# Turning the three-part maximum with a transposing DMA instead of TensorE transposes and a ScalarE copy

## The reference

```
x = x + 0.5 * ffn(layernorm(x))        # 8 routed experts, top 2, plus one shared expert
x = x + attention(layernorm(x))        # causal, linear position bias, softmax
x = x + 0.5 * ffn(layernorm(x))
```

## Time and profile before

| What | Value |
|---|---|
| Runs | 319.05 us median, 316.27 to 319.38 |
| The profiled execution's own time | 317.94 us |
| Its span, first to last instruction | 316.2 us |
| Granted TensorE clock, mean | 0.968 |
| PE busy | 286.5 us, 91% |
| DVE busy | 251.3 us, 79% |
| ACT busy | 175.6 us, 56% |
| POOL busy | 127.7 us, 40% |
| Data moved by DMA | 17.73 MB |

### The profile page before, as it was taken

The page is one execution under the profiler, slowest core; times in us unless marked ns, Lnnn a source line. Parts: engine busy times, 40 slices in busy tenths (PEclk is TensorE's granted clock), DMA queues, the critical chain, the costliest instruction groups (busy, mean ns, idle before and its releaser), DMA issues.

```text
span 316.2 us, 7140 instructions
## 1 busy us (share of the span) xinstructions
PE 286.5 (91%) x2328; PEld 185.6 (59%) x2328; DVE 251.3 (79%) x1039; ACT 175.6 (56%) x342; POOL 127.7 (40%) x251
## 2 busy tenths in 40 slices
PE   0889998999998898999799999999999999999994
PEld 0688886977664343334433344333443799989994
DVE  3799898889787787998778989998621698988875
ACT  2423433433555777878578888886888333334330
POOL 1355256306128623575324534666533352420200
PEclk9999999999997599999889999997999999999999
DMA  6910000660022113411113411110000001000011
GB/s 169 244 24 2 0 0 4 224 167 11 3 101 100 42 51 116 151 54 53 51 40 127 140 54 52 54 55 1 4 2 2 0 3 33 2 18 20 1 32 35
DMA packets 20668, 17.73 MB, mean 56 GB/s; under 512 B 2460, under 2 KB 19420, under 8 KB 20572
## 3 DMA queue, kind: packets, MB, share of 16 engines
q1 hardware_dynamic: 19912, 17.05, 18.0%
q10 hardware_dynamic: 720, 0.23, 0.4%
HBM read 9.74 MB, written 7.34 MB: 54 GB/s over the span
## 4 chain that ended last, share of the span: by engine, by line
PE 61%; DVE 14%; POOL 9%; issue 8%; ACT 4%; DMA 2%; SPq 1%; DVEq 0%; POOLq 0%
PE bank L904 16%; PE bank L1033 10%; PE bank L1001 8%; PE bank L839 6%; PE bank L841 5%; PE bank L840 5%; DVE X L699 4%; POOL probs L402 3%; DVE masked_s L767 2%; PE bank L974 2%; DMA X<-in_x 2%; DVE stats L622 2%; PE bank L1043 2%; ACT probs L528 2%; PE bank L1056 2%
## 5 line engine op out<-in xcount | busy, mean ns | idle before, releaser
L767 DVE CUSTOM_DVE_ANT_0 masked_s<-bank,causal_sb 128x512 f32<-128x512 f32 (+3 forms) x256 | 110.0, 486 | 16.0 <-PE bank L974 15.8
L528 ACT ACTIVATE probs<-bank 128x512 f32<-128x512 f32 x160 | 89.7, 602 | 26.0 <-PE bank L1001 25.1
L699 DVE SCALAR_TENSOR_TENSOR X<-bank,coef,X 128x128 f32<-128x128 f32 x272 | 76.2, 342 | 16.2 <-PE bank L904 13.2
L904 PEld LDWEIGHTS bank<-w_sb,act 128*128 128x128 f32 x512 | 67.3, 192 | 6.6 <-ACT act L451 1.1
L904 PE MATMUL bank<-w_sb,act 128*128 128x128 f32 x512 | 67.7, 275 | 0.6 <-ACT act L451 0.6
L402 POOL TENSOR_SCALAR_AFFINE_SELECT probs<-probs 128x512 f32<-128x512 f32 x64 | 39.8, 635 | 65.5 <-ACT probs L528 65.5
L974 PE MATMUL bank<-KA,QA 54*128 54x512 bf16 (+3 forms) x256 | 59.0, 318 | 4.8 <-DVE smax L767 4.1
L451 ACT ACTIVATE act<-bank 128x512 f32<-128x512 f32 x72 | 41.7, 594 | 37.3 <-PE bank L841 36.7
L1001 PE MATMUL bank<-QA,KA 57*128 57x128 bf16 (+3 forms) x256 | 59.3, 317 | 0.9 <-issue 0.7
L1033 PE MATMUL bank<-probs,VA 128*32 128x256 f32 (+2 forms) x640 | 53.6, 403 | 1.4 <-issue 0.9
L839 PE MATMUL bank<-XH,w_hi 128*128 128x512 f32 x88 | 42.3, 481 | 3.0 <-DVE gated L684 1.8
(11 more groups left out here) (87 smaller groups left out, 334.4 us busy)
## 6 DMA issues: line engine op xcount, KB each, us to landing
qk_scratch<-qk_parts SPq DMA_DIRECT2D x8, 384.0 KB, 2.6
QA<-qk_scratch SPq DMA_DIRECT2D x32, 96.0 KB, 2.2
KA<-qk_scratch SPq DMA_DIRECT2D x32, 96.0 KB, 2.3
qk_scratch<-qk_parts SPq DMA_DIRECT2D x8, 256.0 KB, 2.9
qk_scratch<-qk_parts SPq DMA_DIRECT2D x8, 128.0 KB, 2.8
QA<-smaxT SPq DMA_DIRECT2D x64, 3.0 KB
out_x<-X SPq DMA_DIRECT2D x4, 256.0 KB, 2.3
X<-in_x SPq DMA_DIRECT2D x3, 256.0 KB, 6.1
```

The costliest lines, as they stand in the source:

```text
L528: nc.scalar.activation(dst, src, ACT.Exp).then_inc(exp_done, 1)
L699: m = nc.vector.scalar_tensor_tensor(X[:, b * NT + t, :], Y_BANK[i % 3][:, t * P:(t + 1) * P], coef[:, j % 2, t, n:n + 1], X[:, b * NT + t ...
L767: r = nc.vector.tensor_tensor_reduce(masked_s[:, u % 4, off:off + n], bank[:, off:off + n], causal_sb[:, S - n:S], 1.0, -3e38, ALU.add, AL ...
L904: m = nc.tensor.matmul(Y_BANK[i % 3][:, r], a, w2_sb[:, n, :], start=True, stop=True)
```

## The change

The three parts are laid out as columns 0 to 11 of a 128-wide bf16 tile for each of the four query tiles (`smax3` becomes 128 by 4 by 128, the other 116 columns are set to zero once, on POOL, ahead of the memsets of `VA`). One transposing DMA, issued by SP, turns all 128 by 512 of it into `smaxT`, which becomes 128 by 2 by 4 by 128. The four row DMAs then read 3 of its partitions each. The TensorE transposes, the ScalarE copy and the semaphore between them are removed, and with them one user of the shared PSUM bank. On POOL, `split_smax(n + 2)` moves ahead of the mask of key tile 2, and it now waits for the last transposing DMA (`nmt_sb`) where it waited for PE's transposes. The calls for group 0 in the first feed-forward stage go too; on SP its transposing DMA stands where its row DMAs stood.

```diff
@@ -72,8 +72,8 @@
         VA = [sb(f"VA{i}", [P, NT, H, VW]) for i in range(2)]
         smax = sb("smax", [P, 2, GH, NT])
         smax_rest = sb("smax_rest", [P, GH, NT])
-        smax3 = sb("smax3", [P, NT, GH, PARTS], bf16)
-        smaxT = sb("smaxT", [GH * PARTS, 2, S], bf16)
+        smax3 = sb("smax3", [P, NT, P], bf16)
+        smaxT = sb("smaxT", [P, 2, NT, P], bf16)
         probs = [sb(f"probs{i}", [P, GH, SPAN]) for i in range(2)]
         OT = sb("OT", [P, S])
         rden = sb("rden", [P, NT, GH])
@@ -112,7 +112,7 @@
         aot_ready, at_sb, wo_ready, x_att = sem("aot_ready"), sem("at_sb"), sem("wo_ready"), sem("x_att")
 
         s_ready, s_used = sem("s_ready"), sem("s_used")
-        nm3_ready, nmt_ready, nmt_sb = sem("nm3_ready"), sem("nmt_ready"), sem("nmt_sb")
+        nm3_ready, nmt_sb = sem("nm3_ready"), sem("nmt_sb")
         nm_rows = [sem("nm_rows0"), sem("nm_rows1")]
         t_ready, exp_done, masked = sem("t_ready"), sem("exp_done"), sem("masked")
         pv_ready, ot_sb, ott_ready, ott_used = sem("pv_ready"), sem("ot_sb"), sem("ott_ready"), sem("ott_used")
@@ -251,24 +251,33 @@
                         sp.dma_start(to[b % 2][64 * par:64 * par + PROD, pairs, :],
                                      rows[par][:, :, pairs, :].rearrange("d s pair n -> (d s) pair n")).then_inc(rows_ready[b % 2][g], 16)
 
+            def transpose_smax(G):
+
+                sp.wait_ge(nm3_ready, G + 1)
+                if G >= 2:
+                    sp.wait_ge(nm_rows[G % 2], 64 * (G // 2))
+                sp.dma_start_transpose(smaxT[:, G % 2, :, :], smax3[:, :, :].rearrange("p t c -> p (t c)")).then_inc(nmt_sb, 16)
+
             def maximum_rows(G):
 
                 b, g = divmod(G, NG)
-                sp.wait_ge(nmt_sb, G + 1)
+                sp.wait_ge(nmt_sb, 16 * (G + 1))
                 for hh in range(GH):
                     h = GH * g + hh
                     sp.dma_start(QA[b % 2][64 * (h % 2) + ROWS_S:64 * (h % 2) + ROWS_T, h // 2, :],
-                                 smaxT[PARTS * hh:PARTS * (hh + 1), G % 2, :]).then_inc(nm_rows[G % 2], 16)
+                                 smaxT[PARTS * hh:PARTS * (hh + 1), G % 2, :, :].rearrange("a t q -> a (t q)")).then_inc(nm_rows[G % 2], 16)
 
             write_parts(0, 0)
             write_parts(0, 1)
             for G in range(NG):
                 read_rows(G)
             write_parts(1, 0)
+            transpose_smax(0)
             maximum_rows(0)
             write_parts(1, 1)
             for n in STEPS:
                 if 0 <= n + 1 < NGT:
+                    transpose_smax(n + 1)
                     maximum_rows(n + 1)
                 if n + NG < NGT:
                     read_rows(n + NG)
@@ -373,6 +382,7 @@
             pool.wait_ge(mv_ready, 1)
             inverse_deviation().then_inc(root_ready, 1)
             layer_norm(1, 1)
+            link(nc.gpsimd.memset(smax3[:, :, :], 0.0))
             for i in range(2):
                 link(nc.gpsimd.memset(VA[i][:, :, :, :], 0.0))
             for i in range(2):
@@ -386,13 +396,15 @@
             def split_smax(G):
                 pool.wait_ge(s_used, NU * (G + 1))
                 if G >= 1:
-                    pool.wait_ge(nmt_ready, G)
+                    pool.wait_ge(nmt_sb, 16 * G)
                 m = smax[:, G % 2].rearrange("p h t -> p t h")
                 r = smax_rest[:, :, :].rearrange("p h t -> p t h")
-                link(nc.gpsimd.tensor_copy(smax3[:, :, :, 0], m))
-                link(nc.gpsimd.tensor_tensor(r, m, smax3[:, :, :, 0], ALU.subtract))
-                link(nc.gpsimd.tensor_copy(smax3[:, :, :, 1], r))
-                nc.gpsimd.tensor_tensor(smax3[:, :, :, 2], r, smax3[:, :, :, 1], ALU.subtract).then_inc(nm3_ready, 1)
+                high, middle, low_part = [smax3[:, :, 0:GH * PARTS].rearrange("p t (h a) -> p t h a", a=PARTS)[:, :, :, a]
+                                          for a in range(PARTS)]
+                link(nc.gpsimd.tensor_copy(high, m))
+                link(nc.gpsimd.tensor_tensor(r, m, high, ALU.subtract))
+                link(nc.gpsimd.tensor_copy(middle, r))
+                nc.gpsimd.tensor_tensor(low_part, r, middle, ALU.subtract).then_inc(nm3_ready, 1)
 
             def mask(G, tiles):
                 for kt, need in tiles:
@@ -409,10 +421,10 @@
                 for k in range(2):
                     if (b := projected_at(n, 2 + k)) is not None:
                         low_qk(b, k)
+                if 0 <= n + 2 < NGT:
+                    split_smax(n + 2)
                 if 0 <= n < NGT:
                     mask(n, ((2, 10),))
-                if 0 <= n + 2 < NGT:
-                    split_smax(n + 2)
                 if n == LAST_LN:
                     layer_norm(ln_index(1, B - 1), B - 1)
                 if n == NGT - 6:
@@ -527,12 +539,6 @@
                     dst, src = probs[G % 2][:, head, pos:pos + S], bank[:, :]
                 nc.scalar.activation(dst, src, ACT.Exp).then_inc(exp_done, 1)
 
-            def copy_smax(G):
-                ac.wait_ge(nmt_ready, G + 1)
-                if G >= 2:
-                    ac.wait_ge(nm_rows[G % 2], 64 * (G // 2))
-                nc.scalar.activation(smaxT[:, G % 2, :], MISC[0:GH * PARTS, 0:S // 2].bitcast(bf16), ACT.Copy).then_inc(nmt_sb, 1)
-
             def copy_out(G):
                 ac.wait_ge(pv_ready, G + 1)
                 if G >= 1:
@@ -548,7 +554,7 @@
             PROJECT_ACT = {(1, 5): (split_xt, ln_index(1, 0)), (1, 7): (high_qk, 0, 0), (1, 8): (middle_qk, 0, 0),
                            (2, 0): (high_qk, 0, 1), (2, 1): (middle_qk, 0, 1),
                            (3, 3): (split_xt, ln_index(1, 1)), (3, 4): (high_qk, 1, 0), (3, 5): (middle_qk, 1, 0),
-                           (3, 6): (copy_smax, 0), (3, 7): (high_qk, 1, 1), (3, 8): (middle_qk, 1, 1)}
+                           (3, 7): (high_qk, 1, 1), (3, 8): (middle_qk, 1, 1)}
 
             def load_table(k, function):
 
@@ -570,8 +576,6 @@
                         exps(n, i)
                     if (n, i) in VALUE_SLOTS:
                         values(VALUE_SLOTS.index((n, i)))
-                    if i == 3 and 0 <= n + 1 < NGT:
-                        copy_smax(n + 1)
                     if (b := projected_at(n, 1)) is not None:
                         if i == 9:
                             split_xt(ln_index(1, b))
@@ -979,14 +983,6 @@
                 if len(a) == 1:
                     yield
 
-            def transpose_smax(G):
-                pe.wait_ge(nm3_ready, G + 1)
-                take_misc(nmt_sb, G + 1)
-                dst = MISC[0:GH * PARTS, 0:S // 2].bitcast(bf16)
-                for t in range(NT):
-                    i = nc.tensor.transpose(dst[:, t * P:(t + 1) * P], smax3[:, t, :, :].rearrange("p h a -> p (h a)"), id_b[:, :])
-                i.then_inc(nmt_ready, 1)
-
             def scores_t_steps(G, i):
                 b, g = divmod(G, NG)
                 u = NU * G + i
@@ -1058,7 +1054,7 @@
 
             ln0, ln1 = ln_index(1, 0), ln_index(1, 1)
             PROJECT_PE = {(1, 4): (transpose_xn, ln0, xl_ready, ln0 + 1), (1, 6): (project, 0, 0), (1, 8): (project, 0, 1),
-                          (3, 2): (transpose_xn, ln1, xl_ready, ln1 + 1), (3, 3): (project, 1, 0), (3, 5): (transpose_smax, 0),
+                          (3, 2): (transpose_xn, ln1, xl_ready, ln1 + 1), (3, 3): (project, 1, 0),
                           (3, 6): (project, 1, 1)}
 
             pe.wait_ge(ld_c, 16)
@@ -1075,8 +1071,6 @@
                     score_pair(n, i)
                     if (n, i) in VALUE_SLOTS:
                         values(VALUE_SLOTS.index((n, i)))
-                    if i == 3 and 0 <= n + 1 < NGT:
-                        transpose_smax(n + 1)
                     if i == OUT_SLOT and 0 <= n - 2 < NGT:
                         transpose_out(n - 2)
                     if i in PIECE_SLOTS and 0 <= n - 1 < NGT:
```

## The result

The changed kernel takes 326.25 us (median of 4 runs, 325.08 to 336.38), the kernel before 317.83 (316.27 to 319.38). The ratio is 1.0252, 95% interval 1.02 to 1.0303: slower by 2.5%. Ratios leave out runs that were disturbed on the chip, such as the one at 336.38. The profiled execution took 325.08 us with a span of 323.3, against 317.94 and 316.2.

A forecast was written before the change was run, and what follows sets the result against it. No single engine was the bound: PE, DVE and ACT were near full, the maximum's path tight in five steps. Five steps lose 12.8 us, eleven gain 4.5: +8.3, taken as +8 on 317.94, 326 us; range 313 to 343.

The forecast's parts named there:

- The path of the maximum: From the end of POOL's split through turning and row DMAs to PE's transposed scores; claimed to end last in five steps.
- T: Time of the one transposing DMA from its issue to its landing; taken as 3.9 us, bounds 1.75 to 6.1.
- The sum: Attention steps: five tight ones lose 12.8 us, eleven others gain 4.5, together +8.3; +8 taken.
- the earlier split: POOL's split moved ahead of the mask: starts 0.28 us earlier, some 0.25 taken off the path's growth in a tight step.
- the lateness of SP: SP's row reads and projection writes issued later; rows have about 9 us of cover, so claimed to cost nothing.
- The five tight steps: Steps where PE already waited for row DMAs, 1.6 us in all; each to lose 2.55 us, 12.8 together.
- the reckoning by the loop: Second estimate, over two attention steps: 18.4 us, 9.2 each, 0.28 more than before, +4 over 14 steps; judged too low.
- the freed work: PE's transposes and ACT's copy removed: 0.41 us gained per step where the path does not bind, 4.5 in eleven steps.
- The small parts: Memset under 0.5 us on POOL; mask behind the split, split's wait for the last transposing DMA and SP's later issues: nothing.
- The clock: Idle PE stretches may lower its granted clock, perhaps a microsecond each; left out of the total, kept in the range.
- Hidden: Rival, chance 0.18: no change; transposing DMA near a plain DMA's 2.8 us, steps give +3, 321 us.
- Faster: Rival, chance 0.18: transposing DMA at or under 2.2 us, so freed PE and ACT time decides; about −5, 313 us.

## Why the prediction was right

**The bound.** Right. The path of the maximum was taken to be tight in some steps and the time to follow it. Without T the kernel is 2.2% faster than before, with T twice 11% slower. That only five steps are tight was not right: PE now waits in eight.

**T.** Too large. Sized at 3.9, measured 3.0 in the median (2.5 to 4.4). The row it was taken from, four DMAs issued in series, was the wrong kind; the plain DMA of 128 KB, 2.8, was the nearer. "Advanced Engine Details and Errata" in the Trainium skill, section "X-Bar Transpose (TRN2)", calls the two equally fast, and the trace agrees: 3.0 against 3.1 for the plain DMA of 128 KB in the same profile's list of DMA issues:

```profile
qk_scratch<-qk_parts SPq DMA_DIRECT2D x8, 128.0 KB, 3.1
```

"VectorE: DVE Perf Modes" in the Trainium skill, section "The three transpose paths", gives 1309 ns for a block, from which the prediction made an estimated 5.2 us for four. The trace does not agree with adding it up by the block: four blocks take 2.5 us at best and one block 2.3.

**What T replaced.** The sum put T in the place of 1.10 us. In the kernel before, the handoff (from the end of the split to the first row DMA) is 1.10 us in group 4, but 2.00 in the mean of groups 1 to 15, and 1.42 in the five that wait, since PE and ACT turned the parts only in slot 3. In the changed kernel it is 3.58 in the mean and 3.27 in those five. So the handoff of a tight step grew by 1.85 us where the sum had 2.8 before the earlier split is taken off. The 0.05 us for SP to wake had no row behind it; the changed kernel's shortest lag of SP behind the split is 0.02.

**SP.** Wrong, but it cost little where it counts. I put the lateness of SP at nothing. The transposing DMA was issued 0.6 to 2.2 us after the split in groups 2, 3, 4, 5 and 9, behind SP's row DMAs, reads and writes, 0.46 in the mean of groups 1 to 15. But 4.9 of these 6.9 us lie in groups 2, 5 and 9, for whose rows PE does not wait. In the eight groups that wait, SP's lateness is 2.0 us together, beside 15.5 us of waiting.

**The sum.** That it came out is in good part luck. The five tight steps were to lose 12.8 us; their waits grew by 10.1 (11.7 from 1.6), and three groups that the sum had at nothing wait 3.8 us. Of these 13.9 us the profiled execution gained 7.1 in time, so 6.8 came back, where 4.5 had been reckoned. With the measured T of 3.0 the same sum gives 5 × (3.0 − 1.35) − 4.5 = +3.8, half of what was measured, and the reckoning by the loop gives steps of 8.8 us, a gain, where they last 9.26. T too large by 0.9 stood in for the three further waits and for the slower clock. What the freed work is worth by itself stays loose: 1.7 us by the kernel that puts it back (not clear of noise), 2.4 by the kernel with one block and two row DMAs, whose mean path is 0.2 us shorter than before, and at most 6.9 by the kernel without the DMA, in which the 1.6 us of waits for the rows are gone too.

The step was to last 9.5 us and lasts 9.26: steps 1 to 14 lost 4.4 us. The other 2.7 came before step 1, whose start waits 3.1 us for group 1's rows.

**The small parts.** The earlier split was given 0.28 us a step; the two kernels that undo it or do it alone show none. The memset, the mask behind the split: nothing, as said. The clock was left out of the sum, and that was a term: the granted clock fell from 0.96 to 0.92 in steps 1 to 14, and PE's remaining work there took 3.9 us more, with mean clocks of 0.968 before, 0.939 after and 0.886 with the DMA twice. No experiment held the clock still, so what it adds to the time is not shown by itself. Nor is it shown that the waits lower it: the kernel without the DMA, which waits least for the rows, has 0.953.

**The rivals.** "Hidden" put T near 2.8 and came to +3; T was 3.0, so its T was nearly right, and the time was not: the waits of three more steps and the slower clock are not in its sum either. "Faster" needed a T of about 2.2 or less; no transposing DMA of the changed kernel landed in under 2.5 us, and without the DMA the kernel takes the 313 us that this rival had.

**What stays open.** How much of the loss is the lower clock; how much SP's lateness adds beyond the 2.0 us that lie in waiting groups, since SP, once late, may be late for what it issues next too (no kernel took SP's other work away and left the rest); why the kernel without the DMA is 2% faster than the one with a single PE transpose, when the path of both is short and no more than 0.6 us of waits for the rows is left in either; and why one PE transpose with the earlier split measures 0.8% faster than without it, when the split alone is worth nothing. The last may be no more than the spread of runs, since the intervals touch.

## What to carry to other kernels

Moving work from busy engines to a DMA paid here only where the chain through that work had room for the DMA's latency. Measure from the producer's last instruction to the consumer's first, in every step, and count the steps in which the consumer already waits. Here a microsecond more on that chain in every group cost 4 to 7 us of the kernel's time, and the engine time freed gave 2 to 7. Where the time of a DMA hardly falls with its size, as here, shorten the chain by issuing fewer DMAs behind it rather than smaller ones: two row DMAs in place of four gave 10 us in the changed kernel and a quarter of the bytes nothing that could be told. Where the chain has slack, shortening it gives nothing: in the kernel before, 1.7 us less of it did not show.

## What the hardware showed

The time of a transposing DMA of this size is nearly all fixed. Turning four blocks of 128 by 128 took 2.5 us from issue to landing at best and one block 2.3; its issue on SP took 1.22 and 1.14 us in the median. With four blocks its queue moved 544 packets and 0.13 MB, with one block 160 and 0.03 MB: 128 packets for each block, of some 256 bytes by the difference, and 32 more in both. The DMA queues in the window of group 15, and then of group 14:

```profile
q1 hardware_dynamic: 544, 0.13, 24.9%
...
smaxT<-smax SPq DMA_TRANSPOSE x1, 2.5
```

```profile
q1 hardware_dynamic: 544, 0.13, 15.9%
q8 instruction: 1, 0.02, 1.5%
q14 instruction: 1, 0.01, 0.8%
...
smaxT<-smax SPq DMA_TRANSPOSE x1, 4.0
```

The same 544 packets took 2.5 us alone, and in group 10 also with 250 packets of row reads beside them, and 4.0 with two packets on the instruction queues, one of them of 16 KB. Group 8, with another 600 packets of writes and such a packet beside it, took 4.2. In groups 2, 5, 8, 11 and 14 a 16 KB instruction packet fell in the window, and T was 3.3, 4.1, 4.2, 3.7 and 4.0; in groups 1, 6, 7, 10, 12 and 15, with none, it was 2.5. In groups 3, 4 and 9, beside SP's writes, it was 2.8 to 3.1, in group 13, beside an 8 KB instruction packet, 3.4, and in group 0, right behind three writes, 4.4. No experiment took these packets away, so this is a pattern in the trace and not a shown cause.

A DMA may read 24 partitions of 128 elements and write 3 partitions of 1024: its issue took 0.72 us in the median against 0.64 for a row DMA whose two sides have the same shape.
